# Expert tiles and the joined state-space stage of a decoder in another order on one Trainium2 core

## What is computed

```
x = layernorm(x + attention(x)); x = layernorm(x + cross_attention(x, ctx))
# L0_ffn: one shared expert on all 4096 tokens, and 2 of 8 routed experts for each token
shared = (silu(x @ sg.T) * (x @ su.T)) @ sd.T
p = sigmoid(x @ router.T + bias); top2, idx = top_k(p, 2); top2 /= sum(top2)
routed = sum_k top2[k] * ((silu(x @ wg[idx_k].T) * (x @ wu[idx_k].T)) @ wd[idx_k].T)
x = layernorm(x + shared + routed)
# L1_attn: state-space layer
z, xBC, dt = split(x @ in_proj.T); xBC = silu(causal_conv4(xBC) + conv_b); dt = softplus(dt + dt_bias)
state_t = state_(t-1) * exp(A dt_t) + (x_t dt_t) outer B_t;  y_t = state_t . C_t
y = rmsnorm((y + D x) * silu(z)) * norm_w;  x = layernorm(x + y @ out_proj.T)
x = layernorm(x + causal_cross_attention(x, ctx)); x = layernorm(x + lora_experts(x))
```

## Time and profile before

| | us |
|---|---|
| median of the runs (lowest to highest, 3 runs) | 2969.53 (2964.99 to 2976.01) |
| profiled execution | 2971.47 |
| its span | 2969.7 |
| PE busy in it | 2536.4 (85%) |
| DVE busy | 1857.1 (63%) |
| POOL busy | 1589.0 (54%) |
| ACT busy | 1420.3 (48%) |
| expert tiles in it, from the first transpose to the last output | about 1139 to 1720 |
| joined stage, from the first `gm` to the last | 1802.5 to 2270.4 |

### The profile page before, as it was taken

How to read it: one execution, slowest core, us unless ns; L and a number is a source line. 1 busy time by engine, 2 the same in 40 slices (tenths; PEclk the granted TensorE clock), 3 DMA queues, 4 the chain that set the end, 5 groups by cost and what they waited for, 6 DMA issues and landing times. The chain is left out here.

```text
span 2969.7 us, 66386 instructions
## 1 busy us (share of the span) xinstructions
PE 2536.4 (85%) x24936; PEld 2096.4 (71%) x24936; DVE 1857.1 (63%) x3083; ACT 1420.3 (48%) x2187; POOL 1589.0 (54%) x1809
## 2 busy tenths in 40 slices
PE   5999999996699996999999937778888599995998
PEld 4667666764466666999999926666666377764997
DVE  2666666775477871526666658777785267774665
ACT  2566555653366662335555515444443255553332
POOL 3566656664355430676666655555444477763333
PEclk9899999999799995999999967878887699998999
DMA  7556555541678752136666531101000677752111
GB/s 168 125 141 147 136 126 135 140 112 49 184 195 212 194 125 90 68 133 209 211 213 225 205 109 31 35 29 29 15 12 11 172 188 208 212 141 71 54 53 47
DMA packets 235835, 368.31 MB, mean 124 GB/s; under 512 B 53601, under 2 KB 167009, under 8 KB 228065
## 3 DMA queue, kind: packets, MB, share of 16 engines
q1 hardware_dynamic: 215040, 286.07, 36.4%
q0 software_dynamic: 17376, 78.13, 7.6%
q10 hardware_dynamic: 3200, 1.05, 0.2%
HBM read 236.47 MB, written 137.89 MB: 126 GB/s over the span
## 5 line engine op out<-in xcount | busy, mean ns | idle before, releaser
L1225 ACT ACTIVATE self_probs<-self_score_ps 128x768 f32<-128x768 f32 x256 | 207.6, 811 | 219.1 <-PE self_score_ps L1127 216.1
L1433 POOL TENSOR_SCALAR_AFFINE_SELECT self_probs<-self_probs 128x512 f32<-128x512 f32 x256 | 167.8, 656 | 218.5 <-ACT self_probs L1225 215.8
L2073 POOL TENSOR_TENSOR moee_h_lo<-moee_h,moee_h_hi 128x512 fp32r<-128x512 f32 x110 | 149.8, 1362 | 202.4 <-ACT moee_h_hi L1833 201.5
L1354 DVE TENSOR_REDUCE self_neg_max<-self_max_ps 128x2 f32<-128x256 f32 x256 | 108.0, 422 | 228.0 <-PE self_max_ps L1113 226.8
L672 DVE TENSOR_REDUCE cross_neg_max<-cross_max_ps 128x4 f32<-128x1024 f32 x128 | 155.9, 1222 | 67.6 <-PE cross_max_ps L461 66.0
L589 ACT ACTIVATE cross_probs<-cross_score_ps 128x1024 f32<-128x1024 f32 x128 | 131.1, 1024 | 90.8 <-PE cross_score_ps L483 90.7
L1355 DVE TENSOR_REDUCE self_neg_max<-self_max_ps 128x2 f32<-128x512 f32 x256 | 174.2, 681 | 0.0
L1937 DVE TENSOR_TENSOR moee_in_lo<-moee_in_raw,moee_in_hi 128x2048 fp32r<-128x2048 f32 x40 | 91.7, 2293 | 129.3 <-ACT moee_in_hi L1801 97.4
L1833 ACT ACTIVATE moee_h_hi<-moee_h 128x512 fp32r<-128x512 f32 x110 | 69.6, 632 | 187.6 <-DVE moee_h L1988 187.6
L3171 POOL TENSOR_TENSOR ffn_g_lo<-ffn_g_full,ffn_g_hi 128x512 fp32r<-128x512 f32 x64 | 82.3, 1287 | 142.9 <-ACT ffn_g_hi L3072 142.9
L1127 PE MATMUL self_score_ps<-self_q_stack,self_k_stack 49*128 49x128 f32 (+1 forms) x1024 | 131.4, 336 | 25.1 <-issue 10.6
(11 more groups left out here) (478 smaller groups left out, 9706.4 us busy)
## 6 DMA issues: line engine op xcount, KB each, us to landing
self_q<-self_q_split SPq DMA_DIRECT2D x48, 512.0 KB, 3.2
self_q_raw<-self_q SPq DMA_DIRECT2D x32, 768.0 KB, 7.8
cross_stacks<-cross_qk SPq DMA_DIRECT2D x64, 384.0 KB, 6.5
causal_stacks<-causal_qk SPq DMA_DIRECT2D x64, 384.0 KB, 6.5
moe_y_tiles<-moee_y SPq DMA_DIRECT2D x55, 256.0 KB, 3.0
x_tiles<-zeros SPq DMA_DIRECT2D x16, 624.0 KB, 4.6
moee_x_t<-x_tiles SPq DMA_DIRECT2D x39, 256.0 KB, 3.1
cross_qk<-cross_k_split SPq DMA_DIRECT2D x16, 512.0 KB, 3.9
```

Source lines behind the costliest of these rows:

```text
L1225: nc.scalar.activation(probs[g % 4][:, a, :, P:], score_ps[:, :, P:], ACT.Exp, scale=HD ** -0.5).then_inc(prob_ready, 1)
L1354: dve.tensor_reduce(neg_max[:, tile, :, c, 0:1], bank[:, :, 0:P], AX.X, ALU.max, negate=True)
L1433: pool.affine_select(diagonal, diagonal, [[0, 2], [0, 2], [1, P]], ALU.is_ge, zero, base=0, channel_multiplier=-1).then_inc(prob_masked, 1)
L2073: pool.tensor_tensor(h_lo[p][f][:].rearrange("p j s -> p (j s)"), h[f][:], h_hi[p][f][:].bitcast(F32).rearrange("p j s -> p (j s)"), ALU.s ...
```

## The change

- **Opening.** Four batches (`AHEAD`) are turned before tile 0; the other twelve, with their logits, are put between the products of tiles 0 and 1, two behind each bank (`BETWEEN`). The turned batches stay in SBUF (`xT`), and the shared tiles take `x_hi` and `x_lo` from there, so that their second transposes are gone.
- **Routing** moves to the halves from tile 1 to tile 5; the scatters begin at tile 5, eight in a tile.
- **Shared `h_lo`** goes from POOL to DVE.
- **Routed tiles.** `in_hi` and `in_lo` are made in two halves; `out_hi` and `out_lo` are made in the first half of the step, before `silu` and before `h`; `fetch` on POOL stands behind the first `h_lo` of the step.
- **Joined stage.** The lists of all four engines are rewritten, by even and odd step: one `sum_experts` in each step, other work between `mat`, taps and exponentials, the output product in the bank `xT_ps` in place of `y_ps[0]`, residual and row moments apart, low and high terms and `split_y` signalled in halves.

```
+        AHEAD = 4
+        BETWEEN = {(0, 0, "g"): (4, 5), (0, 0, "u"): (6, 7), (0, 1, "g"): (8, 9), (0, 1, "u"): (10, 11),
+                   (1, 0, "g"): (12, 13), (1, 0, "u"): (14, 15)}
...
-            for b in range(SCANS):
+            for b in range(AHEAD):
                 scan_batch(b)
...
-                    if f == 1 and st.has(1):
+                    if f == 1 and fresh(st, 1):
                         transpose_x(st)
...
# ACT
-                    if f == 0 and fresh(st, 1):
-                        split_in(st)
...
-                    if f == 1 and fresh(st):
+                    if f == 0 and fresh(st):
                         split_out(st)
...
+                        if f == 1 and fresh(st, 1):
+                            split_in(st, 1)
                         act.wait_ge(h_ready, n + 1)
...
+                    if f == 0 and fresh(st, 1):
+                        split_in(st, 0)
...
# DVE
+                    if f == 0 and fresh(st):
+                        lower_out(buffer(st), sets(st))
                     if st.has(0):
                         n = st.at(0) * PAIRS + f
...
-                    if f == 1 and fresh(st):
-                        lower_out(buffer(st), sets(st))
...
                     if shared(st) and st.has(0):
                         route(st.at(0), f)
+                        dve.wait_ge(hhi_ready, n + 1)
...
+                        dve.tensor_tensor(h_lo[p][f][:].rearrange("p j s -> p (j s)"), h[f][:],
+                                          h_hi[p][f][:].bitcast(F32).rearrange("p j s -> p (j s)"),
+                                          ALU.subtract).then_inc(shared_hlo_ready, 1)
...
# POOL
-            FIRST, POINTS = 3, 6
+            FIRST, POINTS = 5, 8
...
-                if fresh(st, 2) or fresh(st, 1):
-                    fetch(st)
                 for f in range(PAIRS):
-                    if st.has(0):
+                    if f == 1 and (fresh(st, 2) or fresh(st, 1)):
+                        fetch(st)
+                    if fresh(st):
                         n = st.at(0) * PAIRS + f
                         pool.wait_ge(hhi_ready, n + 1)
...
# joined stage, PE
-                        last = product3(pe, y_ps[0][:, q * D:(q + 1) * D], (y_hi[:, f, cols], y_lo[:, f, cols]),
+                        last = product3(pe, xT_ps[:, q * D:(q + 1) * D], (y_hi[:, f, cols], y_lo[:, f, cols]),
```

More of the change, by code:

```diff
@@ L2348, in _ @@
[L2348 to L2359 removed]
+                if n % 2 == 0:
+                    if late:
+                        square_sums(n - 1)
+                    project(n, 1)
+                    if now:
+                        exponents(n, 2)
+                        exponents(n, 3)
+                        exponents(n, 4)
+                        exponents(n, 5)
+                    project(n, 2)
+                    if late:
+                        output(n - 1)
+                    if now:
+                        mix(n, 0)
+                    if soon:
@@ L2360, in _ @@
                         to_rows(n + 1)
                     project(n, 3)
-                if now:
-                    mix(n, 0)
-                project(n, 4 if even else 3)
-                if now:
-                    mix(n, 1)
-                if not even:
-                    if real(n + 1):
+                    if now:
+                        mix(n, 1)
+                    if real(n + 4):
+                        transpose_x(n + 4)
+                    project(n, 4)
+                else:
+                    project(n, 0)
+                    if now:
+                        exponents(n, 2)
+                        exponents(n, 3)
+                    project(n, 1)
+                    if late:
+                        square_sums(n - 1)
+                    if now:
+                        exponents(n, 4)
+                        exponents(n, 5)
+                    if late:
+                        output(n - 1)
+                    project(n, 2)
+                    if now:
+                        mix(n, 0)
+                        mix(n, 1)
+                    if real(n + 4):
+                        transpose_x(n + 4)
+                    project(n, 3)
+                    project(n, 4)
+                    if soon:
@@ L2510, in _ @@
-                if not even:
-                    gate_z(n, 3)
         def matrices(eng, n, u, ready):
@@ L2723, in _ @@
                     if now:
-                        skip_terms(n, 0)
-                if now:
-                    skip_terms(n, 1)
-                    gated(n)
-                if not even:
+                        tail_rows(n)
+                        matrices(dve, n, 0, low_mat_ready)
+                    if late:
+                        mean_squares(n - 1)
+                    taps(n, 0)
+                    taps(n, 1)
+                    if now:
+                        matrices(dve, n, 2, low_mat_ready)
+                        matrices(dve, n, 4, low_mat_ready)
@@ L2733, in _ @@
                 if real(n + 4):
[L2734 to L2737 removed]
+                    lower_x(n + 4)
         @block.gpsimd
```

452 lines of the change are left out of this document (258 added, 194 removed).

## The result

The changed kernel is slower: 3069.86 us median (3062.86 to 3072.86, 4 runs) against 2970.94 us (2964.99 to 2976.01), a ratio of 1.033 with a 95% interval of 1.0304 to 1.0357. The forecast was 3004, with a range to 3070: the direction was right, the size was not (+99 us where +34 was forecast).

A forecast was written before the change was run, and what follows sets the result against it. PE was taken to bound opening, shared and routed tiles, DVE's waits to matter in the joined stage. Front -9, routed loop +126, joined stage -82 sum to +35 on 2971.5; with the median 1.9 lower, 3004 us, range 2942 to 3070.

The forecast's parts named there:

- What bounds the kernel: Whole kernel: PE bounds opening, shared and routed tiles; no engine is full in the joined stage, where DVE's waits matter.
- The routed loop: Routed tiles: `fetch` and early `out_hi` close a loop through the transfer, 13.06 us a tile against 9.68; +126 us.
- `row` to the issue of `out_raw` 1505.04 to 1506.91, 1.87: Routed tiles: POOL's step within the 13.06 us round, put at 1.87 us from one round of the old trace.
- 0.1 us, in idle time: Routed tiles: estimated cost to ACT and DVE, each, of one more fixed start from splitting `in` in halves.
- Rival 1: Routed tiles: `out_raw` lands in 4.1 us, not 6.0; round 11.16 us, sum -37, 2933 us; chance 0.12.
- Rival 4: Routed tiles: idle PE falls to the low clock, 16.2 us a tile, up to +119, 3123 us; chance 0.08.
- The front: Opening and shared tiles up to tile 16: -29 + 29.4 + 7 - 16, about -9 us (from -30 to -3).
- where tile 16 begins at 11 x 8.7 = 96: Shared tiles: 8.7 us each from tile 5 to 16, so first routed weights, about 94 us behind, are just hidden.
- The joined stage: Joined stage: work put ahead of waits removes four fifths of DVE's 103.1 us of waits for ACT; -82 us.
- rival 3: Joined stage gains little, -30 us, because late results on POOL hold PE, ACT, then DVE; +87, 3056 us; chance 0.20.
- The least that a pair can take is DVE's 51.13 us: Joined stage: floor for a pair of steps, against 67.67 us before; at most 8 x 16.5 = 132 us gained.
- The chances: Whole kernel's time: faster 0.16, same 0.15, slower 0.69; the forecast itself 0.45.

The follow-up runs named there:

- e10: e2 without the 64 scatters and SP's wait for them, so the routed tiles run over rows of zeros: 2839.95 us.
- e1: The changed kernel with `fetch` ahead of both `h_lo` again, `out_hi` and `out_lo` staying in the first half of the step: 2895.55 us.
- e2: The changed kernel with `out_hi` and `out_lo` back in the second half of the step, `fetch` staying behind the first `h_lo`: 2879.77 us.
- e7: The changed kernel with the two DMAs in `fetch` swapped, `out_raw` issued ahead of `in_raw`: 2937.35 us.
- e5: e2 with three scatters behind each half tile in place of four, beginning at tile 4: 2866.62 us.
- e9: e2 with seven scatters a tile, four behind the first half and three behind the second, from tile 5 on: 2861.72 us.

## Why the prediction missed its size

- **What bounds the kernel** was read rightly for the routed tiles and the joined stage. For the shared tiles it was not: I read "PE bound" from 148.93 of 157 us, where the last tiles ran at POOL's 10.0 us. It did not change the sum: the 8.7 us that were put in are PE's, and e10 shows 8.64.
- **The routed loop** (+126 forecast, +174.8 measured) is the term that failed, in its size; the mechanism was right, and e1 and e2 open the loop from either side. The step that failed is "`row` to the issue of `out_raw` 1505.04 to 1506.91, 1.87". That price was read in a round in which DVE did nothing with two SBUF inputs at that place. In the new order `in_lo` stands right there in every round, and the step costs 3.32 us in the mean, 1.45 more. The landing was right (6.05 in the mean), and `h_lo` was 0.2 shorter than put in. Within 0.1 us that gives the 1.22 us by which the pitch is longer than 13.06: 38 x 1.22 = 46 of the 49 us. The trace of the kernel before had the warning in it: the step takes some 4.0 us in every second of its rounds (the rows at 1496.19 above), and its mean over 37 of them is 2.93 us, 1.06 above the one that was read. The text put the cost of the halves of `in` at "0.1 us, in idle time"; DVE's idle time it was, but POOL's working time.
- **Rival 1** (the short landing) did not come: the median of `out_raw` stayed at 6.0. In e7, where `out_raw` goes first, it lands in 4.3 and the time, 2937 us, is near the rival's 2933, but that is partly luck: the landing gives 1.7 of the 3.4 us a round, the rest is the other issue and `row`. By the fit of the Trainium skill (DMA: Bandwidth & Descriptors, "Anatomy of one DMA — SWDGE (gpsimd) path"), the landing would have been an estimated 4.3 behind the second issue; the trace has 6.0 there.
- **Rival 4** (the clock) came in half: PEclk fell to 0.86 in the routed tiles, but PE still waited 125 us for `x_lo`, and the pitch moved with the terms of the loop (14.28, 13.29, 13.25, 10.84) and went to 9.11 when it was opened. It swung within the tile: in the round shown it is 0.50 from 1507.3 to 1513.0, behind a wait of 3.54 us, and 1.00 from 1516.0 on. The Trainium skill (TensorE: Matmul & The Clock Gate, "HAM oscillation — how this bites in real kernels") tells of such a clock, which falls in every pass that waits for a transfer, and the trace agrees. It did not set the time here.
- **The front** (-9 forecast, +4.2 measured) is two misses of opposite sign. Until `x_hi` of tile 5 the change gained 6.0 us where the working gives a loss of 4: the two tiles with the batches in between took less than 29.4 + 7 us more, because the clock was not low all the way (0.57 from 1140 to 1181). This part is uncertain by the 10 us by which traces of the same work differ there. From tile 5 to 16 it lost 10.2 where -13 stood in the sum ("where tile 16 begins at 11 x 8.7 = 96"): e10 shows those 96 us, without the scatters, and 25 more with them. The sum counted eight scatters a tile as POOL's work alone and left out what they do to PE, which is the second term that failed.
- **The joined stage** (-82 forecast, -72.7 measured, -77 alone) was right in its direction and near in size, the size partly by luck. Of the waits for ACT even more went than the four fifths taken (98.4 us to 14.3), but waits for PE grew from 2.9 to 33.4 and took part of it back, as in rival 3, only smaller. That left 55 us. The other 17.5 are DVE's shorter instructions, of which the sum had nothing. For the same reason "The least that a pair can take is DVE's 51.13 us" did not hold: in the pair from 2027.46 to 2081.91 DVE is busy for 45.88.
- The chances put 0.69 on slower, and the time lay at the very edge of the range. The bounds of the routed term, +101 to +155, held only the landing and `h_lo`; no bound was worked out for POOL's small steps.

## What to carry to other kernels

Before a prefetch is moved, follow what its issue waits for and what its data releases: if the same chain is on both sides, the transfer's whole latency is paid in every pass, and moving either end, or swapping two issues, opens or shortens it. Price the steps of such a loop where they will stand, with the work that will run beside them, and over many rounds: one round of a trace can be the cheap half of a pattern that alternates. And where a long queue of indirect scatters runs beside dense matmuls, spread it: here it cost 25 us, though no engine was full while it did.

## What was not expected of the hardware

A 128x2 instruction of POOL takes 1.18 us instead of 0.19 if it starts while a DVE subtraction of two SBUF operands runs, and 2.33 beside one that is twice as long; it ends some 0.05 us behind that. The issue of an indirect DMA that starts there takes 1.78 instead of 0.96, but one that is already under way is not longer. Scatters issued every 1.27 us over stretches of several tiles make PE stop for 0.2 to 1.0 us between matmuls with all operands there, and in the changed kernel the granted clock was 0.50 for some 3 us behind a group of them: a tile of 8.64 us takes 12. That the stops come from the scatters is shown by e10, that they shrink with spacing by e5 and e9; by which path a scatter holds PE's instructions is open.
